# Moving the shifted feed-forward input's transfers behind the scores, and its layer-norm statistics later, in a software-pipelined attention kernel

## The chip, the cores and the metric

The kernel runs on one core of one Trainium2 chip. The metric is the device time of one execution, in microseconds (us). The core has these engines: PE (TensorE, matrix products), DVE (VectorE), ACT (ScalarE), POOL (GpSimd) and SP (SyncE, which here issues nearly all DMA transfers). "PEld" in the profile is PE's weight load, which overlaps its matmuls. Each engine works through its own list of instructions in order; between engines only semaphores order the work, and an engine that waits for one holds up everything behind the wait in its own list.

## What is computed

The input is 2 x 1024 tokens of width 128. The work is: a stack of 6 transformer layers on the normalized input, half of it added; a small recurrent layer in the middle; and the same stack of 6 layers once more. One layer of the stack is (reference, cut down):

```python
def shift_tokens(t):                      # second half of the channels comes from the token before
    a, s = jnp.split(t, 2, -1)
    s = jnp.pad(s, ((0, 0), (1, 0), (0, 0)))[:, :-1]
    return jnp.concatenate([a, s], -1)

def attn_layer(x, Wqkv, qs, ksc, Wo):     # 16 heads of 64, windows of 32 keys looking one window back
    q, k, v = split(x @ Wqkv)
    q, k = l2norm(q) * qs, l2norm(k) * ksc
    q, k = rotary(q), rotary(k)           # with xpos scales
    return local_attention(q, k, v) @ Wo

def ffn_layer(x, g, bln, W1, b1, W2, b2):
    mu = x.mean(-1, keepdims=True)
    var = ((x - mu) ** 2).mean(-1, keepdims=True)
    xn = (x - mu) / jnp.sqrt(var + 1e-05) * g + bln
    hg = xn @ W1 + b1
    a, gate = jnp.split(hg, 2, -1)
    return a * jax.nn.gelu(gate, approximate=False) @ W2 + b2

for i in range(DEPTH):
    x = attn_layer(shift_tokens(x), ...) + x
    x = ffn_layer(shift_tokens(x), ...) + x
```

## The kernel before, in words

The tokens are cut into 16 tiles of 128 (a tile is one SBUF block of 128 partitions), and the residual stream of all of them stays in SBUF, in `Z`. There are 12 layers of 16 tiles, so 192 tile-layers ("tiles" from here on). The program is one software pipeline over these: a *step* is a turn of the pipeline, and in step s the stages work on different tiles. Stage `L_X` (transpose of the input) works on tile s, `L_QKV` on tile s-1, `L_S` (keys, values, scores) on s-2, `L_SM` (softmax) on s-3, `L_AV` and `L_WO` (attention output, output projection) on s-4, `L_F` (first half of the feed-forward part) on s-5 and `L_F2` (its second half) on s-6. All steps are written out, without loops. `k.wait(sem, lag)` waits until the semaphore has counted the tile s-lag; `k.on(lag)` says whether that stage has a tile in this step.

Within a step, each engine's list is written out by hand:

- **PE** (`step`, lines 544 to 658): q/k projection chunks 1 and 0 (L484), transposes of the rotated q (L495), attention times values (L539, 64 matmuls), projection chunks 2 and 3, transposes of the rotated k, output projection (L594), transposes of the probabilities (L602), the transpose of the normalized feed-forward input `xn` (L607, it waits for `a_xn` from ACT), the second feed-forward product (L622), the value projections 1 and 0 (L490), the transpose of the layer's input (L639), the first feed-forward product (L503), and last the scores: the mask (L519) and 128 small matmuls (L527). The last of these signals `p_S`.
- **DVE** (lines 919 to 1021): rotary products of chunks 0 and 1 (L861 and L867, each twice), the row sums of the softmax (L940) and their reciprocals (L949, signals `v_rec` to POOL), sums of squares (L954, L957), the rotary products of chunks 3 and 2, a chain of small operations for the reciprocal square root of the norms (L816 to L848), the two residual additions (L969, signals `v_z1`; L979), a copy of transposed probabilities (L992), the gated product `hT` (L1001), the maximum of the scores (L1008, waits for `p_S`) and their subtraction (L1011, signals `v_sub`).
- **ACT** (lines 679 to 755): squares of chunks 1 and 0 (L673), exponentials (L686), copies of transposed q (L691) and attention output (L695), squares 3 and 2, the copy of transposed k (L711), **`xn`** (L715, waits for `v_nb` from DVE), the copy of transposed probabilities (L722), `xnT` (L727), two value copies (L677), the gelu (L740) and the three parts of the transposed input `xsT` (L747, L748, L750; `a_xT`). PE's first projection of the next step waits for `a_xT`.
- **POOL** (lines 1070 to 1095): the small power for the layer norm (L1074, waits for `v_ve`, signals `g_rstd`), the multiplication of the probabilities by the reciprocals (L1078, waits for `v_rec`, signals `g_nrm` to PE's transposes L602), two additions of rotary products (L1084), a table (L1058), two multiplications by the norms (L1093).
- **SP** (lines 436 to 458): two transfers of the values to `vb` (L447, L448, behind `p_O`), two loads of the next layer's weights in every second step (L357, L361), and the *shift* of the feed-forward input: four transfers (L405 to L408) from `Z` to `xs2`, whose second half of the channels goes down by one partition. They wait for `v_z1` of tile s-4. Each counts 16 on `d_xs2`.

The layer-norm statistics of `xs2` are these: `bn_stats` (L1016) at the end of DVE's list, for tile s-4, behind `d_xs2`; in the next step `bn_aggr` (L932, between the rotary products of chunk 1), the addition of epsilon (L937, signals `v_ve`), POOL's power (L1074), and `nb`, the product of mean and reciprocal deviation (L945, signals `v_nb`), between the row sums and their reciprocals. Then ACT makes `xn` and PE transposes it.

Of the kernel before, what the change touches and what calls it, by code (L numbers as in the profile page):

```python
# [57 lines left out]
def macaron(nc, x_in, w_in, w_out, b_out, w_qkv, q_scale, k_scale, w_o,  # L58
            w_1, w_2, b_2, c_cols, c_rope, c_mask, c_ident, out):
    with ExitStack() as ctx:  # L60
# [293 lines left out]
        def _(sp):  # L354
# [46 lines left out]
            def shift(k, lag, dst, sm):  # L401

                hf, cut = P // 2, P - 16
                new, tail, left = k.slot(lag), k.slot(lag, 0, hf), k.slot(lag, 1, hf)
                sp.dma_start(dst[:, 0:hf], Z[:, bass.ds(new, hf)]).then_inc(sm, 16)  # L405
                sp.dma_start(dst[1:cut + 1, hf:P], Z[0:cut, bass.ds(tail, hf)]).then_inc(sm, 16)
                sp.dma_start(dst[cut + 1:P, hf:P], Z[cut:P - 1, bass.ds(tail, hf)]).then_inc(sm, 16)
                sp.dma_start(dst[0:1, hf:P], Z[P - 1:P, bass.ds(left, hf)]).then_inc(sm, 16)  # L408
# [27 lines left out]
            def step(k):  # L436
                if k.reg is not None:

                    for lag in (L_X, L_WO):
                        k.slot(lag), k.slot(lag, 0, P // 2), k.slot(lag, 1, P // 2)  # L440
                if k.on(L_SM):


                    k.wait(a_v[0], L_SM)
                    k.wait(p_O, L_AV)
                    par = k.parity(L_SM)
                    sp.dma_start(vb[WIN:P, :], va[0:P - WIN, par, :]).then_inc(d_vb, 16)  # L447
                    sp.dma_start(vb[0:WIN, :], va[P - WIN:P, 1 - par, :]).then_inc(d_vb, 16)  # L448
                load_weights(k)
                if k.on(L_WO):  # L450


                    k.wait(v_z1, L_WO)
                    shift(k, L_WO, xs2[:, :], d_xs2)
                if k.reg is None and k.s >= OUT:
                    t = k.s - OUT
                    sp.wait_ge(f_out, t + 1)
                    sp.dma_start(out[t // POS, (t % POS) * P:(t % POS + 1) * P, :], xb[:, t, :]).then_inc(d_out, 16)
# [9 lines left out]
        def _(pe):  # L468
# [75 lines left out]
            def step(k):  # L544
# [52 lines left out]
                if k.on(L_SM):  # L597
# [3 lines left out]
                    for p in range(PAIRS):  # L601
                        last = tr(tps[:, p, :], prob[:, p, :, :].rearrange("p a b -> p (a b)"), idf[:, :])  # L602
                    last.then_inc(p_pT, 1)
                if k.on(L_F):
                    k.wait(a_xn, L_F)
                    k.wait(v_sub, L_S + 1)
                    tr(sps[:, 1, 0:P], xn[:, :], idf[:, :]).then_inc(p_xnT, 1)  # L607
                if k.on(L_F2):
                    if k.reg is None and k.s == L_F2:
                        pe.wait_ge(d_late, 16 * len(late_consts))  # L610
                    k.wait(v_h, L_F2)
                    k.wait(a_oT, L_AV)
                    if k.mid(M_IN) is not None:
                        k.wait_mid(m_xT, M_IN)
                        mm(ops[:, 1, 0:P], winT[:, :], mx_t[:, :], start=True, stop=True, skip_group_check=True)
                    if k.mid(M_OUT) is not None:
                        k.wait_mid(m_y, M_OUT)
                        mm(ops[:, 1, P:2 * P], ys[:, k.mid(M_OUT) % 2, :], woutT[:, :], start=True, stop=True,
                           skip_group_check=True)
                    at = k.layer(L_F2, 3 * P)  # L620
                    for c in range(3):
                        last = mm(ops[:, 1, 3 * P:4 * P], hT[0:FC, c, :], w2[0:FC, bass.ds(at + c * P, P)],  # L622
                                  start=(c == 0), stop=(c == 2))
                    last.then_inc(p_f2, 1)
                if k.on(L_S):
                    weights(k, L_S, d_wq, CHUNKS)
                    k.wait(v_ab[3], L_QKV)
                    values(k, 1)
# [154 lines left out]
        def _(dve):  # L783
# [135 lines left out]
            def step(k):  # L919
                if k.on(L_QKV):  # L920
# [3 lines left out]
                        k.wait(g_tab, L_QKV, base=-1)  # L924
                    rotate(k, 0, True)
                    rotate(k, 0, False)
                if k.on(L_F):
                    k.wait(v_bn, L_F)
                if k.on(L_QKV):
                    rotate(k, 1, True)  # L930
                if k.on(L_F):
                    v.bn_aggr(mv[:, :], st[:, :]).then_inc(v_mv, 1)  # L932
                if k.on(L_QKV):
                    rotate(k, 1, False)
                if k.on(L_F):
                    k.wait(v_mv, L_F)
                    v.tensor_scalar(rt2[:, 0:1], mv[:, 1:2], 1e-5, None, ALU.add).then_inc(v_ve, 1)  # L937
                if k.on(L_SM):
                    k.wait(a_exp, L_SM)
                    v.tensor_reduce(rs[:, :], prob[:, :, :, :].rearrange("p a t j -> p (a t) j"), AX,  # L940
                                    ALU.add).then_inc(v_sum, 1)
                if k.on(L_F):
                    k.wait(g_rstd, L_F)
                    k.wait(a_xn, L_F + 1)
                    v.tensor_scalar(nb[:, 0:1], mv[:, 0:1], rt2[:, 1:2], -1.0, ALU.mult, ALU.mult).then_inc(v_nb, 1)  # L945
                if k.on(L_SM):
                    k.wait(v_sum, L_SM)
                    k.wait(g_nrm, L_SM + 1)
                    v.reciprocal(rr[:, :], rs[:, :]).then_inc(v_rec, 1)  # L949
                if k.on(L_QKV):  # L950
                    k.wait(a_sq[0], L_QKV)
                    k.wait(v_sub, L_S + 1)
                    k.wait(v_rs, L_QKV + 1, per=RS_STEPS)
                    v.tensor_reduce(xsq[:, 0:HEADS], heads(sq[:, 0:INNER]), AX, ALU.add).then_inc(v_red[0], 1)  # L954
                    rotate(k, 3, True)
                    k.wait(a_sq[2], L_QKV)
                    v.tensor_reduce(xsq[:, HEADS:2 * HEADS], heads(sq[:, INNER:2 * INNER]), AX, ALU.add).then_inc(v_red[1], 1)  # L957
                    rotate(k, 3, False)
                    rsqrt(k, 1)
                    rotate(k, 2, True)  # L960
                    rsqrt(k, 2)
                    rotate(k, 2, False)
                    rsqrt(k, 4)
# [41 lines left out]
                if k.on(L_S):  # L1005
# [5 lines left out]
                    v.tensor_tensor(prob[:, :, :, :].rearrange("p a t j -> p t a j"), s4,  # L1011
                                    mx[:, :].rearrange("p (t a) -> p t a", t=2).unsqueeze(3)
                                    .to_broadcast([P, 2, PAIRS, 2 * WIN]), ALU.subtract).then_inc(v_sub, 1)
                if k.on(L_WO):
                    k.wait(d_xs2, L_WO, per=64)
                    v.bn_stats(st[:, :], xs2[:, :]).then_inc(v_bn, 1)  # L1016
                if k.reg is None and k.on(L_F2) and k.tile(L_F2) >= T - TILES:

                    t = k.tile(L_F2) - (T - TILES)
# [33 lines left out]
        def _(pool):  # L1053
# [14 lines left out]
            scl2 = scl[:, :, :, :].rearrange("p l k d -> p (l k d)")  # L1068

            def step(k):  # L1070
                if k.on(L_F):
                    k.wait(v_ve, L_F)
                    k.wait(a_xn, L_F + 1)
                    g_.tensor_tensor(rt2[:, 1:2], rt2[:, 0:1], half[:, 0:1], ALU.pow).then_inc(g_rstd, 1)  # L1074
                if k.on(L_SM):
                    k.wait(v_rec, L_SM)
                    pr = prob[:, :, :, :].rearrange("p a t j -> p (a t) j")
                    g_.tensor_tensor(pr, pr, rr[:, :].unsqueeze(2).to_broadcast([P, HEADS, 2 * WIN]),  # L1078
                                     ALU.mult).then_inc(g_nrm, 1)
                if k.on(L_QKV):  # L1080
                    for g in range(2):
                        k.wait(v_ab[1 + g], L_QKV)
# [147 lines left out]
```

## Time and profile before

| | |
|---|---|
| median of 3 runs | 3302.99 us (3298.94 to 3304.68) |
| the profiled execution's own time | 3302.78 us |
| its span in the trace | 3301.0 us |
| mean granted clock of PE | 0.994 |
| instructions | 125954 |
| busy share of the span | PE 96%, PEld 72%, DVE 91%, ACT 77%, POOL 68% |

The span is the time between the first and the last recorded instruction of this one execution; 1.8 us of its time lie outside it. A busy share is an average over the whole program. A matmul's end is modelled in the trace, so a busy PE is not always a PE at its peak; in rows of several merged instructions the busy time runs from the first start to the last end. "A <- B" in the waits means that the engine at A stood still until B was done; "issue" stands for a wait that the trace ascribes to nothing.

### The profile page before, as it was taken

The numbers are of one execution on the slowest core, as the hardware profiler recorded it, in microseconds if no ns is written. First come the engines' busy times: TensorE is split into PE (matmuls) and PEld (weight loads), VectorE is DVE, ScalarE is ACT, GpSimd is POOL, SyncE is SP. The second block draws the span as 40 slices with busy tenths as digits, with TensorE's granted clock in tenths as the row PEclk, the third lists the DMA queues.
The fourth block names the chain that finished last, engine by engine and source line by source line (L and its number), as shares of the span: only waits on it lengthen the run. The fifth ranks groups of instructions, "written<-read, shape, count | busy, mean of one in ns | idle before, by whom it ended". The sixth has DMA issues, their size and how long they took to land. (4 is left out here: it accounts for less than half of the span.)

```text
span 3301.0 us, 125954 instructions
## 1 busy us (share of the span) xinstructions
PE 3177.7 (96%) x50984; PEld 2377.1 (72%) x51176; DVE 2994.8 (91%) x7143; ACT 2543.2 (77%) x4144; POOL 2229.6 (68%) x1454
## 2 busy tenths in 40 slices
PE   7999999999999999999889999999999999999998
PEld 3777777777777777776667777777777777777776
DVE  7999999999899999999999998899999999999995
ACT  3877878777787777777667777788777777887775
POOL 6666666666666666667777766666666666666663
PEclk9999999999999999999999999999999999999999
DMA  4111111111111111111111111111111111111111
GB/s 124 44 48 44 48 45 48 45 48 44 47 45 48 45 48 45 47 44 39 37 37 47 45 48 45 40 48 46 45 44 48 45 48 45 48 45 48 47 52 38
DMA packets 134996, 155.84 MB, mean 47 GB/s; under 512 B 75539, under 2 KB 108439, under 8 KB 134423
## 3 DMA queue, kind: packets, MB, share of 16 engines
q1 hardware_dynamic: 129815, 144.42, 15.9%
q8 instruction: 413, 6.77, 0.9%
q10 hardware_dynamic: 4608, 3.34, 0.4%
q14 instruction: 160, 1.31, 0.1%
HBM read 33.38 MB, written 1.05 MB: 10 GB/s over the span
## 5 line engine op out<-in xcount | busy, mean ns | idle before, releaser
L1084 POOL TENSOR_TENSOR rot<-rot,swp 128x1024 f32<-128x1024 f32 x384 | 907.2, 2363 | 132.5 <-DVE rot L867 132.5
L484 PE MATMUL proj<-wq,xsT 128*128 128x512 f32 x1536 | 773.4, 622 | 55.9 <-DVE hT L1001 22.4
L673 ACT ACTIVATE sq<-proj 128x512 f32<-128x512 f32 x768 | 437.6, 596 | 400.6 <-PE proj L484 387.3
L1093 POOL TENSOR_TENSOR rot<-rot,rn 128x1024 f32<-128x1024 f32 x384 | 724.6, 1910 | 0.0
L1074 POOL TENSOR_TENSOR rt<-rt,half 128x1 f32<-128x1 f32 x192 | 105.8, 551 | 743.1 <-DVE rt L937 743.1
L861 DVE TENSOR_TENSOR swp<-proj,tab 128x512 f32<-128x512 f32 x768 | 522.0, 680 | 9.4 <-ACT sq L673 5.1
L867 DVE TENSOR_TENSOR rot<-proj,tab 128x512 f32<-128x512 f32 x768 | 518.9, 676 | 1.7 <-PE tps L495 1.6
L495 PEld LDWEIGHTS tps<-idf,rot 128*128 128x128 f32 x3072 | 362.6, 141 | 207.1 <-issue 205.1
L1078 POOL TENSOR_TENSOR prob<-prob,rr 128x1024 f32<-128x1024 f32 x192 | 365.8, 1905 | 174.7 <-DVE rr L949 174.7
L484 PEld LDWEIGHTS proj<-wq,xsT 128*128 128x128 f32 x1536 | 257.5, 189 | 293.0 <-issue 138.1
L495 PE MATMUL tps<-idf,rot 128*128 128x128 f32 x3072 | 402.0, 274 | 3.5 <-POOL rot L1093 1.9
L594 PE MATMUL ops<-wo,oT 128*128 128x128 f32 x3072 | 376.3, 276 | 4.0 <-ACT oT L695 4.0
L539 PE MATMUL ops<-pT,vb 128*64 128x64 f32 x6144 | 379.3, 225 | 0.0
L490 PE MATMUL proj<-wq,xsT 128*128 128x512 f32 x768 | 369.5, 601 | 3.5 <-DVE rot L867 3.3
L539 PE MATMUL ops<-pT,va 128*64 128x64 f32 x6144 | 369.6, 222 | 0.0
L594 PEld LDWEIGHTS ops<-wo,oT 128*128 128x128 f32 x3072 | 359.8, 193 | 4.3 <-issue 4.2
L527 PEld LDWEIGHTS sps<-kT,qT 64*32 64x32 f32 x24576 | 258.4, 105 | 121.5 <-issue 121.1
L722 ACT COPY pT<-tps 64x1024 f32<-64x1024 f32 x192 | 193.2, 1006 | 187.3 <-PE tps L602 187.3
L1001 DVE SCALAR_TENSOR_TENSOR hT<-proj,cols,fg 114x128 f32<-114x128 f32 (+1 forms) x576 | 166.8, 345 | 187.4 <-issue 179.1
L539 PEld LDWEIGHTS ops<-pT,vb 128*64 128x64 f32 x6144 | 311.6, 138 | 32.9 <-issue 32.6
L527 PE MATMUL sps<-kT,qT 64*32 64x64 f32 x24576 | 296.2, 225 | 33.3 <-issue 33.2
L503 PEld LDWEIGHTS proj<-xnT,w 128*114 128x114 f32 (+1 forms) x2304 | 273.5, 178 | 73.7 <-issue 67.9
(104 smaller groups left out, 6164.6 us busy)
## 6 DMA issues: line engine op xcount, KB each, us to landing
vb<-va SPq DMA_DIRECT2D x192, 384.0 KB, 3.5
vb<-va SPq DMA_DIRECT2D x192, 128.0 KB, 3.6
wq<-in_L_ffn_Wqkv SPq DMA_DIRECT2D x95, 192.0 KB, 3.4
xs<-Z SPq DMA_DIRECT2D x192, 32.0 KB
wo<-in_L_ffn_Wo SPq DMA_DIRECT2D x94, 64.0 KB, 2.8
xs<-Z SPq DMA_DIRECT2D x192, 28.0 KB
xs<-Z SPq DMA_DIRECT2D x192, 3.8 KB
xs<-Z SPq DMA_DIRECT2D x192, 0.2 KB
```

What stands on the lines that cost most here:

```text
L484: mm(proj[:, c % 2, :], xsT[:, k.parity(L_QKV), 0:P], wq2[:, bass.ds(w + c * 512, 512)], start=True, stop=True).then_inc(p_qkv[c], 1)
L490: mm(proj[:, c, :], xsT[:, k.parity(L_S), 0:P], wq2[:, bass.ds(w + (4 + c) * 512, 512)], start=True, stop=True).then_inc(p_v[c], 1)
L495: last = tr(tps[:, p, :], rot[:, g * INNER + p * P:g * INNER + (p + 1) * P], idf[:, :])
L527: last = mm(sps[to:to + WIN, ty, p * 64:(p + 1) * 64], qT[rows, p, w * WIN:(w + 1) * WIN], kT[rows, p, at:at + 2 * WIN], start=False, stop ...
L539: last = mm(o4[hp * DH:(hp + 1) * DH, :, g, :], v, pT[:, 2 * p + g, hp, :, :].rearrange("p t i -> p (t i)"), start=True, stop=True, skip_g ...
L594: last = mm(ops[:, 0, 0:P], oT[:, p, :], wo[:, bass.ds(w + p * P, P)], start=(p == 0), stop=(p == PAIRS - 1))
L673: fn(sq[:, c * 512:(c + 1) * 512], proj[:, c % 2, :], ACT.Square).then_inc(a_sq[c], 1)
L861: v.tensor_tensor(halves(swp[:, c * 512:(c + 1) * 512]), swapped, tab[:, bass.ds(po + (2 * g + 1) * POS * DH, DH)] .rearrange("p (a d) -> ...
L867: v.tensor_tensor(heads(rot[:, c * 512:(c + 1) * 512]), heads(src), tab[:, bass.ds(po + 2 * g * POS * DH, DH)].unsqueeze(1) .to_broadcast( ...
L1078: g_.tensor_tensor(pr, pr, rr[:, :].unsqueeze(2).to_broadcast([P, HEADS, 2 * WIN]), ALU.mult).then_inc(g_nrm, 1)
L1084: g_.tensor_tensor(r, r, swp[:, g * INNER:(g + 1) * INNER], ALU.add).then_inc(g_add[g], 1)
L1093: g_.tensor_tensor(r, r, rn[:, g * HEADS:(g + 1) * HEADS].unsqueeze(2) .to_broadcast([P, HEADS, DH]), ALU.mult).then_inc(g_nm[g], 1)
```

## The change

On SP the shift waits for `p_S` of tile s-2 as well, so its four transfers are issued when the scores of the step are done. On PE the transpose of `xn` goes behind the second feed-forward product. On DVE `bn_stats` goes from the end of the step to the next step, behind the four rotary products of chunks 0 and 1 (it now waits for `d_xs2` there); `bn_aggr` comes behind the row sums, the epsilon behind the reciprocals, and `nb` behind the rotary products of chunk 3. On POOL the power comes behind the multiplication of the probabilities.

```diff
@@ SP, step
                     k.wait(v_z1, L_WO)
+                    k.wait(p_S, L_S)
                     shift(k, L_WO, xs2[:, :], d_xs2)
@@ PE, step
-                if k.on(L_F):
-                    k.wait(a_xn, L_F)
-                    k.wait(v_sub, L_S + 1)
-                    tr(sps[:, 1, 0:P], xn[:, :], idf[:, :]).then_inc(p_xnT, 1)
                 if k.on(L_F2):
...
                     last.then_inc(p_f2, 1)
+                if k.on(L_F):
+                    k.wait(a_xn, L_F)
+                    k.wait(v_sub, L_S + 1)
+                    tr(sps[:, 1, 0:P], xn[:, :], idf[:, :]).then_inc(p_xnT, 1)
@@ DVE, step
                     rotate(k, 0, False)
-                if k.on(L_F):
-                    k.wait(v_bn, L_F)
-                if k.on(L_QKV):
                     rotate(k, 1, True)
-                if k.on(L_F):
-                    v.bn_aggr(mv[:, :], st[:, :]).then_inc(v_mv, 1)
-                if k.on(L_QKV):
                     rotate(k, 1, False)
                 if k.on(L_F):
-                    k.wait(v_mv, L_F)
-                    v.tensor_scalar(rt2[:, 0:1], mv[:, 1:2], 1e-5, None, ALU.add).then_inc(v_ve, 1)
+                    k.wait(d_xs2, L_F, per=64)
+                    v.bn_stats(st[:, :], xs2[:, :]).then_inc(v_bn, 1)
                 if k.on(L_SM):
                     k.wait(a_exp, L_SM)
                     v.tensor_reduce(rs[:, :], prob[:, :, :, :].rearrange("p a t j -> p (a t) j"), AX,
                                     ALU.add).then_inc(v_sum, 1)
                 if k.on(L_F):
-                    k.wait(g_rstd, L_F)
-                    k.wait(a_xn, L_F + 1)
-                    v.tensor_scalar(nb[:, 0:1], mv[:, 0:1], rt2[:, 1:2], -1.0, ALU.mult, ALU.mult).then_inc(v_nb, 1)
+                    k.wait(v_bn, L_F)
+                    v.bn_aggr(mv[:, :], st[:, :]).then_inc(v_mv, 1)
                 if k.on(L_SM):
                     k.wait(v_sum, L_SM)
                     k.wait(g_nrm, L_SM + 1)
                     v.reciprocal(rr[:, :], rs[:, :]).then_inc(v_rec, 1)
+                if k.on(L_F):
+                    k.wait(v_mv, L_F)
+                    v.tensor_scalar(rt2[:, 0:1], mv[:, 1:2], 1e-5, None, ALU.add).then_inc(v_ve, 1)
...
                     rotate(k, 3, False)
+                if k.on(L_F):
+                    k.wait(g_rstd, L_F)
+                    k.wait(a_xn, L_F + 1)
+                    v.tensor_scalar(nb[:, 0:1], mv[:, 0:1], rt2[:, 1:2], -1.0, ALU.mult, ALU.mult).then_inc(v_nb, 1)
+                if k.on(L_QKV):
                     rsqrt(k, 1)
...
-                if k.on(L_WO):
-                    k.wait(d_xs2, L_WO, per=64)
-                    v.bn_stats(st[:, :], xs2[:, :]).then_inc(v_bn, 1)
@@ POOL, step
-                if k.on(L_F):
-                    k.wait(v_ve, L_F)
-                    k.wait(a_xn, L_F + 1)
-                    g_.tensor_tensor(rt2[:, 1:2], rt2[:, 0:1], half[:, 0:1], ALU.pow).then_inc(g_rstd, 1)
                 if k.on(L_SM):
                     k.wait(v_rec, L_SM)
...
                                      ALU.mult).then_inc(g_nrm, 1)
+                if k.on(L_F):
+                    k.wait(v_ve, L_F)
+                    k.wait(a_xn, L_F + 1)
+                    g_.tensor_tensor(rt2[:, 1:2], rt2[:, 0:1], half[:, 0:1], ALU.pow).then_inc(g_rstd, 1)
```

## Rows read from the trace of the kernel before

**Rows 1.** The page, busy time, share of the span and instructions of each engine.

```profile
PE 3177.7 (96%) x50984; PEld 2377.1 (72%) x51176; DVE 2994.8 (91%) x7143; ACT 2543.2 (77%) x4144; POOL 2229.6 (68%) x1454
```

**Rows 2.** Two stretches: length; busy us (count) of PE, PEld, DVE, ACT, POOL; PEclk, DMA.

```profile
900.00:1200.00 300.00, 295.38 (x4804) 222.31 (x4819) 274.91 (x653) 240.46 (x390) 203.50 (x127) 1.00 0.17 46
...
1500.00:1800.00 300.00, 273.60 (x4125) 202.55 (x4135) 293.68 (x704) 211.08 (x350) 220.05 (x179) 0.98 0.15 41
```

**Rows 3.** Timeline of steady steps, around PE: start, us, engine, line, operation.

```profile
1004.80 0.68 DVE L867 TENSOR_TENSOR rot<-proj,tab 128x512 f32<-128x512 f32 x1
...
1005.62 0.27 PE L607 MATMUL sps<-idf,xn 128*128 128x128 f32 x1
...
1022.15 0.27 PE L607 MATMUL sps<-idf,xn 128*128 128x128 f32 x1
...
1022.26 0.83 PE L622 MATMUL ops<-w,hT 114*128 114x128 f32 x6
...
1026.76 1.48 PE L527 MATMUL sps<-kT,qT 64*32 64x64 f32 x128
...
1028.05 0.20 ACT L750 ACTIVATE xsT<-xsT 64x1 f32<-64x1 f32 x1
...
1028.35 1.95 PE L484 MATMUL proj<-wq,xsT 128*128 128x512 f32 x4
```

**Rows 4.** Timeline of a steady step, DVE's order from the scores on.

```profile
1012.10 1.23 DVE L1008 TENSOR_REDUCE mx<-sps 128x16 f32<-128x1024 f32 x1
...
1014.01 0.60 ACT L673 ACTIVATE sq<-proj 128x512 f32<-128x512 f32 x1 [0.20 <-PE proj L484]
1014.50 0.28 DVE L1016 BATCH_NORM_STATS2 st<-xs 128x6 f32<-128x128 f32 x1
...
1014.70 0.69 DVE L861 TENSOR_TENSOR swp<-proj,tab 128x512 f32<-128x512 f32 x1
...
1016.59 0.66 DVE L867 TENSOR_TENSOR rot<-proj,tab 128x512 f32<-128x512 f32 x1
...
1018.35 0.21 DVE L945 TENSOR_SCALAR nb<-mv,rt 128x1 f32<-128x1 f32 x1
1018.47 0.25 DVE L949 RECIPROCAL rr<-rs 128x16 f32<-128x16 f32 x1
...
1021.44 0.68 DVE L867 TENSOR_TENSOR rot<-proj,tab 128x512 f32<-128x512 f32 x1
...
1022.04 0.19 DVE L816 TENSOR_SCALAR sps<-sps 128x32 f32<-128x32 f32 x1
```

**Rows 5.** The same step: POOL, and ACT's `xn` and value copies; waits in brackets.

```profile
1017.39 0.55 POOL L1074 TENSOR_TENSOR rt<-rt,half 128x1 f32<-128x1 f32 x1 [3.85 <-DVE rt L937]
...
1018.80 1.90 POOL L1078 TENSOR_TENSOR prob<-prob,rr 128x1024 f32<-128x1024 f32 x1 [0.86 <-DVE rr L949]
...
1020.74 0.52 ACT L715 ACTIVATE xn<-xs,nb,rt 128x128 f32<-128x128 f32 x1
...
1024.06 0.59 ACT L677 COPY va<-proj 128x512 f32<-128x512 f32 x1 [0.35 <-PE proj L490]
...
1024.85 0.59 ACT L677 COPY va<-proj 128x512 f32<-128x512 f32 x1 [0.19 <-PE proj L490]
```

**Rows 6.** SP's transfers: timeline of a steady step.

```profile
1016.96 0.52 SPq L447 DMA_DIRECT2D vb<-va  x1
...
1023.93 0.51 SPq L405 DMA_DIRECT2D xs<-Z  x1
...
1026.01 0.55 SPq L408 DMA_DIRECT2D xs<-Z  x1
```

**Rows 7.** DMA issues: count, KB each, median us from issue to landing.

```profile
vb<-va SPq DMA_DIRECT2D x192, 384.0 KB, 3.5
...
out<-xb SPq DMA_DIRECT2D x16, 64.0 KB, 1.8
```

**Rows 8.** Waits of the whole run: us in total, times, longest.

```profile
DVE mx L1008 <- PE sps L527: 34.2, 34, 2.7
```

## The prediction

> **What bounds the kernel now.** I read the busy shares first. PE is busy 96% of the span, DVE 91%, ACT and POOL well below [rows 1]. Since these are averages, I then read them by stretch. In a steady stretch PE is busy 295.4 of 300 us at full granted clock and DVE 274.9. In the middle, where the recurrent layer is worked in between, DVE is at 293.7 of 300 and PE at 273.6 [rows 2]. So about 176 of the 192 steps belong to PE and about 16 to DVE.
>
> Next I read the timeline of steady steps. PE's two feed-forward transposes L607 are 1022.15 - 1005.62 = 16.5 us apart, which is one step [rows 3]. PE has almost no gap within it, save one at its end: the scores end at 1026.76 + 1.48 = 1028.24, ACT's last part of the transposed input ends at 1028.05 + 0.20 = 1028.25, and PE's next projection starts at 1028.35 [rows 3]. PE thus goes on when ACT has ended, 0.10 us after it. ACT's work ahead of that (value copy, table load, gelu, three copies) starts from PE's value projections. The loop that sets the step is therefore PE from the projections to the values, and from there PE and ACT side by side. The reader should see two things in it: work that only DVE, POOL or SP gain does not shorten a step, and whatever delays PE ahead of its value projections lengthens the step by as much, since ACT's branch starts later too.
>
> **The change, part by part.** All sums are made against the profiled execution, 3302.8 us (span 3301.0 and 1.8 around it), which lies 0.2 us under the median of the runs, so one figure serves for both.
>
> *DVE, the removed bn_stats at the end of the step.* It takes 1014.70 - 1014.50 = 0.20 us from start to start. The rotary product behind it can't move up by that much: it also needs ACT's square, which ends at 1014.01 + 0.60 = 1014.61; with 0.05 us for the signal it starts at 1014.66 in place of 1014.70 [rows 4]. Gain 0.04 us, and it is DVE's alone.
>
> *DVE, up to the last rotary product of chunk 3 (L867 at 1021.44).* bn_stats is added ahead of it (0.20), nb is taken from there (1018.47 - 1018.35 = 0.12), bn_aggr and the epsilon only change places. So that product shifts by -0.04 + 0.20 - 0.12 = +0.04 us [rows 4]. DVE's reciprocals shift by less than 0.05 too: ahead of them bn_stats (0.20) comes, and nb (0.12) and the epsilon, the shorter of the two, go. POOL's multiplication of the probabilities then keeps its place.
>
> *POOL, the power behind the multiplication.* The latter ends at 1018.80 + 1.90 = 1020.70, the power takes 0.55, so g_rstd comes at 1021.25 [rows 5]. nb now stands where L816 starts, at 1022.04, so it finds g_rstd done 0.8 us earlier. POOL's two rotary additions behind it start up to 0.55 us later; POOL is busy 203.5 of 300 us [rows 2] and has that room. Cost nothing; if the 0.8 us were gone, the nb below would be late by the rest.
>
> *nb, xn and PE's transpose: the costly part.* nb starts 0.60 us behind the start of L867 (1022.04 - 1021.44) and takes 0.21; ACT follows after some 0.06, xn takes 0.52, and PE follows 0.10 behind it as above [rows 3 to 5]. From the start of L867 that is 0.04 + 0.60 + 0.21 + 0.06 + 0.52 + 0.10 = 1.53 us. PE's slot for the transpose has moved too, behind six matmuls of (0.83 - 0.28)/5 = 0.11 us each: it comes 0.67 us behind the place of today's L607 [rows 3]. In the one step the transpose is due at 1022.15 + 0.67 = 1022.82 and its input is there at 1021.44 + 1.53 = 1022.97: PE waits 0.15 us. In the other kind of step (every second one has an additional copy on ACT, and PE runs 0.1 us later against DVE) it is due at 1005.62 + 0.67 = 1006.29, the input at 1004.80 + 1.53 = 1006.33: 0.04 us. The mean is 0.095 us, and 176 steps make 17 us. Before, xn was made at 1020.74, a good microsecond ahead of its use, so this cover of PE is what the later statistics take away. Bounds for this term: if all signals come at once (0.06 + 0.10 left out), nothing waits, 0 us; if a weight load of 0.11 us is exposed on top, 0.205 x 176 = 36 us.
>
> *ACT, the later xn.* xn now ends at about 1022.87, and the copy of the probabilities, xnT and the value copies stand behind it. That chain would come some 0.5 us later, but it had waits of 0.35 and 0.19 us for the value projections in it [rows 5], which take that up. I put this at nothing beyond PE's wait; it is inside the upper bound above.
>
> *SP, the shift behind the scores.* Four issues take 1026.01 - 1023.93 + 0.55 = 2.63 us [rows 6]. They now run from 1012.10, where the scores are done [rows 4], to 1014.7; the next thing on SP, the vb transfer at 1016.96 [rows 6], is not held up. The weight loads stand ahead of the shift and stay. When do the transfers land? The last one is issued 2.1 us behind the first, and no row gives its landing: the nearest are 1.8 us (64 KB) and 3.5 us (384 KB) [rows 7], so 3.9 to 5.6 us after the first. bn_stats is due on DVE at 1014.66 + (1016.59 - 1014.70 - 0.09) + 0.57 = 1017.03, 0.09 being bn_aggr that left, so 4.9 us behind 1012.10 [rows 4]. It waits for nothing at the lower end and for 0.7 us at the upper. I take the lower end for most steps, as the transfers are small (at most 32 KB) and thus nearest to the 64 KB row, and the middle, 0.3 us, for those in which something is in the way; as a count of these I take the 34 steps in which PE stopped in the scores for something other than data [rows 8]. That is 10 us, and since nb and xn stand behind bn_stats, it goes to PE in full. Bounds: 0, and 0.7 x 176 = 123 us.
>
> *PE's stops in the scores.* In 34 steps DVE waited 34.2 us in all for the scores [rows 8], 1 us at a time, while these 128 small matmuls went out. The shift's transfers fly just then, at 1023.9 to about 1028 against scores at 1026.8 to 1028.2. If they are the cause, the change gives up to 34 us back. The rows show only that the two are together, so I take nothing: in five of six steps they are together as well and nothing stops. The Trainium skill says in *Runtime: NRT & Kernel Launch*, "Instruction fetch mechanics", that crossing a block of 16 KiB of code costs little and is mostly hidden; by it there would be no such stops, and the trace, with its 34.2 us, disagrees. By that page alone this term would be nothing as well.
>
> *The middle's 16 steps.* DVE's total of work is the same; bn_stats is not late there, since a step lasts longer. Nothing, with 2 us either way.
>
> The sum is +17 + 10 = +27 us: 3302.8 + 27, about 3330.
>
> **The rivals.** *A, forecast: xn reaches PE late.* For it: the path from L867 to the transpose is made of measured parts, and has 0.04 to 0.15 us too little time. Against it: the margin is as small as a signal. 3330; by its bounds 3310 to 3350.
>
> *B: the transfers land late in most steps.* DVE would stand 0.3 to 0.7 us ahead of bn_stats in each step, and PE with it: 0.3 x 176 = 53 us or more on top of A's 17, so 3373 and up. For it: the upper landing row of 3.5 us. Against it: the size of the transfers. It decides from a landing 4.9 us behind the first issue.
>
> *C, faster: the stops in the scores go.* All 34.2 us come back, less A's 17: 3286; with xn on time, 3269. The Trainium skill (*DMA: Bandwidth & Descriptors*, "Queues, rings and completion order") says that a DMA engine takes turns between its queues by whole packets; by that rule a code load does wait behind the shift's packets, and moving them away makes it land earlier. For it: the stops fall exactly on the time of the transfers. Against it: the scores are also the place where PE takes most instructions per microsecond (128 matmuls and their loads in 1.5 us), which alone explains why it would run dry there.
>
> *D: no change.* The signals are quick enough, xn is there in time, and nothing else lies on the loop: 3303, within 6.6 us.
>
> **How the numbers follow.** 0.2% (6.6 us) is about what a measurement of this kernel tells from no change. A 0.56, B 0.10, C 0.18, D 0.16. A's lowest end and D's highest meet, so "same" is 0.16 and slower 0.66. The predicted time is A's. The range takes in A with its bounds, D, the half of C in which only part of the stops goes or A's cost eats it (above 3292), and the beginning of B: 3292 to 3366. For A alone it is 3310 to 3350.
>
> **What would show it.** In the changed profile, PE's or PEld's wait at L607 for ACT's xn should appear with some 15 us in total (it is 4 us in one startup step now), and PE's busy time in a steady 300 us should fall or its count of matmuls with it, by 0.6%. DVE's wait at bn_stats for the transfers would be some tens of steps with 0.1 to 0.7 us; in most steps if B is right. The wait of DVE's maximum for the scores should stay near 34 us; if it falls to a few, C is right. POOL's power should wait less in total, being behind the multiplication. The prediction is wrong if L607 waits for nothing, or if the gap ahead of the next step's projection absorbs what L607 costs.

## The result, and the profile after

The changed kernel takes 3348.3 us (median of 4 runs) against 3303.8 for the kernel before: ratio 1.0139, 95% interval 1.0121 to 1.0156. It is 44 us slower, clear of the noise; the forecast was slower by 27 us, 3330 in a range from 3292 to 3366. The kernel before was run again beside the experiments, and its median there lies between 3304.6 and 3305.5; times are compared with these. All ratios are of fast executions, which leaves out one execution of 7018.6 us, of the run that shortens DVE's stretch.

First the page's busy shares and the two stretches of the windows view after (the columns are those of [rows 1] and [rows 2]):

```profile
PE 3224.6 (96%) x51176; PEld 2380.6 (71%) x51176; DVE 3026.7 (90%) x7143; ACT 2542.8 (76%) x4144; POOL 2222.4 (66%) x1454
```

```profile
900.00:1200.00 300.00, 294.71 (x4772) 218.90 (x4772) 273.00 (x642) 235.20 (x385) 201.88 (x126) 1.00 0.17 45
1500.00:1800.00 300.00, 272.99 (x4131) 201.45 (x4130) 291.34 (x683) 207.14 (x341) 212.52 (x174) 0.95 0.14 38
```

PE's busy share is the same as in [rows 1] although it does the same work in a longer time. The two busy times can't be compared: the trace before lacks 192 matmul records of PE, those of the mask (50984 against 51176). The weight loads are complete in both (51176), so their number in a stretch is the better measure. In the steady stretch it is 4772 against 4819 before [rows 2], 1% fewer, at the same granted clock.

The waits of the whole run after (us in total, times, longest):

```profile
POOL prob L1073 <- DVE rr L943: 1016.4, 192, 13.4
...
ACT xn L716 <- DVE nb L959: 282.1, 192, 4.4
...
PEld proj L491 <- DVE rot L868: 110.0, 186, 1.1
...
DVE mx L1010 <- PE sps L528: 35.6, 37, 2.9
...
PEld sps L625 <- ACT xn L716: 31.6, 107, 1.5
...
DVE st L932 <- DMA xs<-Z: 13.2, 26, 1.7
...
PE sps L625 <- ACT xn L716: 10.6, 28, 1.3
```

ACT now waits in each step for nb, and in 107 steps PE's load waits for xn in turn, as forecast. In 26 steps bn_stats waits for the transfers, 0.5 us each (the line `DVE st <- DMA xs<-Z`). PE's stops in the scores are what they were: 35.6 us against 34.2 [rows 8].

A steady step after, in the timeline, DVE with the rows of the other engines that meet it:

```profile
1030.10 0.60 ACT L674 ACTIVATE sq<-proj 128x512 f32<-128x512 f32 x1 [0.20 <-PE proj L485]
...
1030.78 0.69 DVE L862 TENSOR_TENSOR swp<-proj,tab 128x512 f32<-128x512 f32 x1
...
1033.18 0.28 DVE L932 BATCH_NORM_STATS2 st<-xs 128x6 f32<-128x128 f32 x1
...
1034.79 0.10 DVE L946 TENSOR_SCALAR rt<-mv 128x1 f32<-128x1 f32 x1
1034.82 1.23 DVE L951 TENSOR_REDUCE sps<-sq 128x16 f32<-128x1024 f32 x1
...
1036.81 0.55 POOL L1078 TENSOR_TENSOR rt<-rt,half 128x1 f32<-128x1 f32 x1
...
1037.68 0.68 DVE L868 TENSOR_TENSOR rot<-proj,tab 128x512 f32<-128x512 f32 x1
1038.28 0.21 DVE L959 TENSOR_SCALAR nb<-mv,rt 128x1 f32<-128x1 f32 x1
...
1038.52 0.49 ACT L716 ACTIVATE xn<-xs,nb,rt 128x128 f32<-128x128 f32 x1 [1.57 <-DVE nb L959]
1039.06 0.14 PEld L625 LDWEIGHTS sps<-idf,xn 128*128 128x128 f32 x1 [0.19 <-ACT xn L716]
...
1039.29 0.68 DVE L868 TENSOR_TENSOR rot<-proj,tab 128x512 f32<-128x512 f32 x1
...
1040.02 0.30 PEld L491 LDWEIGHTS proj<-wq,xsT 128*128 128x128 f32 x2 [0.59 <-DVE rot L868]
```

The path of the forecast is there link by link: the last rotary product of chunk 3 at 1037.68, nb at 1038.28, xn at 1038.52, PE's load at 1039.06. But a second one lies beside it. The last rotary product of chunk 2, at 1039.29 to 1039.97, releases PE's load for value projection 0 at 1040.02. From DVE's first rotary product of the step to this one it is 1039.29 - 1030.78 = 8.51 us. Before it was 8.23 us: from 1014.70 [rows 4] to 1022.93, which is this row of the timeline before:

```profile
1022.93 0.68 DVE L867 TENSOR_TENSOR rot<-proj,tab 128x512 f32<-128x512 f32 x1
```

One step can mislead, so here are medians over the same 144 steps of each run's trace (72 on either side of the middle, away from the start and the end). The *stretch* runs from the end of ACT's last square ahead of DVE's first rotary product to the start of the last product of chunk 2. The *step* is the time from one such product to the next; steps of two kinds alternate, and both are given. The runs are those of the experiments below.

| run | stretch, us | step, us (two kinds) |
|---|---|---|
| shortened stretch | 8.08 | 16.34 / 16.44 |
| **before** | 8.37 | 16.37 / 16.45 |
| changed, bn_stats back at the end, shift ahead of the scores | 8.45 | 16.45 / 16.45 |
| before, one more bn_stats at the end | 8.56 | 16.56 / 16.56 |
| before, one more bn_stats behind the products | 8.56 | 16.55 / 16.55 |
| changed, shift ahead of the scores | 8.59 | 16.58 / 16.58 |
| **changed** | 8.59 | 16.59 / 16.58 |
| changed, bn_stats behind the row sums | 8.73 | 16.71 / 16.71 |

In every line but the first, a step takes the stretch and 7.99 us more, within 0.01 us; before, that holds for one kind of step, and the other takes 0.08 us longer than that. So DVE's stretch already set the pace of every second step in the kernel before, and had 0.08 us to spare in the others. In the changed kernel it sets the pace of both kinds: they are 0.22 and 0.14 us longer, 0.18 in the mean, and 0.18 x 176 = 31 us of the 44. The forecast had PE and ACT as the only loop.

### The profile page after: what moved, and what is told of

It is laid out like the page before. It is cut to its first block and busy times, and to the rows that moved or that the text cites. A ratio compares the mean times of both kernels' runs of the same rounds, so it can differ in the third digit from the quotient of the medians.

```text
span 3348.5 us, 126338 instructions
## 1 busy us (share of the span) xinstructions
PE 3224.6 (96%) x51176; PEld 2380.6 (71%) x51176; DVE 3026.7 (90%) x7143; ACT 2542.8 (76%) x4144; POOL 2222.4 (66%) x1454
## 5 line engine op out<-in xcount | busy, mean ns | idle before, releaser
L504 PE MATMUL proj<-xnT,w 128*114 128x128 f32 (+1 forms) x2304 | 311.9, 285 | 2.3 <-ACT xnT L728 1.8
L540 PEld LDWEIGHTS ops<-pT,va 128*64 128x64 f32 x6144 | 312.6, 138 | 0.0
```

The source lines that it names most:

```text
L504: last = mm(proj[0:rows, a, c * P:(c + 1) * P], w1[:, at + a * FH + c * FC:at + a * FH + c * FC + rows], xnT[:, :], start=True, stop=True, ...
L540: last = mm(o4[hp * DH:(hp + 1) * DH, :, g, :], v, pT[:, 2 * p + g, hp, :, :].rearrange("p t i -> p (t i)"), start=True, stop=True, skip_g ...
```

## The experiments

Theory A, the forecast's, was that the late xn costs the time. Its rivals were the place in PE's list (O), the late transfers (L), and PE's stops in the scores (C). All ratios are to the kernel before.

**PE's order alone.** In the kernel before, only this:

```diff
@@ PE, step
-                if k.on(L_F):
-                    k.wait(a_xn, L_F)
-                    k.wait(v_sub, L_S + 1)
-                    tr(sps[:, 1, 0:P], xn[:, :], idf[:, :]).then_inc(p_xnT, 1)
                 if k.on(L_F2):
...
                     last.then_inc(p_f2, 1)
+                if k.on(L_F):
+                    k.wait(a_xn, L_F)
+                    k.wait(v_sub, L_S + 1)
+                    tr(sps[:, 1, 0:P], xn[:, :], idf[:, :]).then_inc(p_xnT, 1)
```

> Before, with PE's transpose of xn alone moved behind the second feed-forward product; everything else as before. Theory A (what costs is that xn comes late from DVE and ACT): xn ends about 1.5 us ahead of its new slot, so PE waits for nothing and the time stays at 3303 +- 5. Rival O (the new place in PE's list costs something by itself: in the changed kernel the place took 0.046 us more ahead of it and 0.056 us more behind it even in the steps without a wait): 0.10 us in each of 176 steps, so 3321.

3308.2 us, ratio 1.0007 (0.9998 to 1.0016). The place costs at most some 5 us; rival O's 18 us fall. In the medians over steps, as in the table, the stretch and both kinds of step are those of the kernel before.

**nb one instruction earlier,** in the changed kernel:

```diff
@@ DVE, step
+                    v.tensor_scalar(nb[:, 0:1], mv[:, 0:1], rt2[:, 1:2], -1.0, ALU.mult, ALU.mult).then_inc(v_nb, 1)
                     rotate(k, 3, False)
-                    v.tensor_scalar(nb[:, 0:1], mv[:, 0:1], rt2[:, 1:2], -1.0, ALU.mult, ALU.mult).then_inc(v_nb, 1)
```

> After, with DVE's nb one instruction earlier, ahead of the last rotary product of chunk 3 (0.6 us) in place of behind it. Theory A: xn ends 0.6 us earlier and PE never waits for it, except where bn_stats itself waited for the transfers; PE's 0.22 us per step go, 39 us in all, save some 5 for the transfers: 3310 to 3316. Rival O: the place in PE's list keeps its 18 us: about 3330. Rival L (the late transfers make the most of it): 3340 or more.

3349.0 us, 1.0134 (1.0120 to 1.0148): nothing gained. That is against theory A and rival O, and inside rival L's "3340 or more", which the next run takes up. Its waits:

```profile
PEld proj L491 <- DVE rot L868: 151.3, 188, 1.1
...
DVE st L932 <- DMA xs<-Z: 13.1, 19, 1.9
...
PEld sps L625 <- ACT xn L716: 2.8, 2, 2.5
```

The wait for xn is gone (31.6 to 2.8 us), and the wait of the very next group of PE's list, the value projections, for DVE's rotary product has grown from 110.0 to 151.3 us, by as much and more. So xn was the first of two waits of about the same length, both behind the same work of DVE. Theory A falls as a theory of the cause. What took its place is theory D: DVE's work between ACT's square and the rotary product of chunk 2 has grown, and this stretch is on the loop.

**The shift ahead of the scores again,** in the changed kernel:

```diff
@@ SP, step
-                    k.wait(p_S, L_S)
                     shift(k, L_WO, xs2[:, :], d_xs2)
```

> After, without SP's wait for the scores; the statistics and PE's order stay as in after. Theory A: DVE's 13 us of waits for the transfers go, and they stood on PE's path: 3335 to 3340. Rival L: 3320 or less. Rival C (the shift's transfers, when they fly with the scores, hold up PE's code): PE's stops in the scores would be longer than in after, so the gain would be given back, 3348 or more.

3336.3 us, 1.0096 (1.0081 to 1.0112): 12 us come back, against 13.2 us of waits for the transfers. Rival L (3320 or less) falls: the late transfers are not the most of it. Rival C falls too, since nothing is given back. The waits for the scores:

```profile
DVE mx L1009 <- PE sps L527: 29.1, 25, 3.0
```

**Both,** in the changed kernel, with the two diffs above:

> After, with both: nb ahead of the last rotary product of chunk 3, and SP's wait for the scores left out. Theory A: neither wait is left, 3303 to 3307. Rival O: 3321. If something third makes the change slow (POOL's or DVE's order), it shows here as what is left above 3303.

3335.1 us, 1.0094 (1.0080 to 1.0108). With neither wait of the forecast left, 30 us of the 44 remain. "Something third" it is. It shows in this wait:

```profile
PEld proj L490 <- DVE rot L867: 144.1, 187, 1.1
```

against 104.0 us before: 40 us more. These are waits of PE's loads, which run ahead of its matmuls, so they tell where PE is held up but are not added up to the time.

**bn_stats back at the end of the step,** in the changed kernel with the shift ahead of the scores; the rest stays:

```diff
@@ DVE, step
                     rotate(k, 1, False)
-                if k.on(L_F):
-                    k.wait(d_xs2, L_F, per=64)
-                    v.bn_stats(st[:, :], xs2[:, :]).then_inc(v_bn, 1)
...
+                if k.on(L_WO):
+                    k.wait(d_xs2, L_WO, per=64)
+                    v.bn_stats(st[:, :], xs2[:, :]).then_inc(v_bn, 1)
```

> After, with SP's wait for the scores left out (as in the run without it, 3336) and bn_stats back at the end of DVE's step; aggregate, epsilon, nb, POOL's order and PE's order stay as in after. Theory D (bn_stats costs because it now stands in DVE's work between ACT's square and the rotary product of chunk 2, which PE's value projection and xn both wait for): 0.2 us of DVE's work leave that stretch, so the 30 us left go, 3303 to 3308. Rival G (the later aggregate, epsilon and power on DVE and POOL make the cost): it stays at about 3330.

3315.1 us, 1.0030 (1.0020 to 1.0041). 21 us of the 31 go with this one instruction; 10 stay. So D holds for the larger part, and a part of G's is there too, though neither gave 3315. Where? The timeline of this run:

```profile
1002.94 0.17 DVE L935 BATCH_NORM_AGGREGATE mv<-st 128x2 f32<-128x6 f32 x1
1003.05 0.25 DVE L939 RECIPROCAL rr<-rs 128x16 f32<-128x16 f32 x1
1003.23 0.10 DVE L942 TENSOR_SCALAR rt<-mv 128x1 f32<-128x1 f32 x1
1003.25 1.23 DVE L947 TENSOR_REDUCE sps<-sq 128x16 f32<-128x1024 f32 x1
1004.39 0.68 DVE L861 TENSOR_TENSOR swp<-proj,tab 128x512 f32<-128x512 f32 x1
```

and the same sum of squares over the whole of its run, then in the kernel before (the view of one line; ns, min/median/max):

```profile
L947 DVE TENSOR_REDUCE sps<-sq x192: 1168/1228/1230, 16.3 to 3258.9; 128x16 f32<-128x1024 f32 x192
```

```profile
L954 DVE TENSOR_REDUCE sps<-sq x192: 1168/1169/1218, 16.3 to 3242.9; 128x16 f32<-128x1024 f32 x192
```

The epsilon stands right ahead of the sum of squares now; the next instruction starts 0.02 us behind it, but the sum takes 59 ns more than where it stood behind the reciprocals. Where in DVE's list a small instruction stands changes what its neighbours take. The whole stretch is 0.08 us longer than before (8.45 against 8.37). That lengthens only those steps that had nothing to spare: 0.04 us in the mean, 7 us in 176 steps. The 18 steps around the middle, where DVE is the bound, took 349.2 us in this run's trace and 342.6 before (one trace each). The two make somewhat more than the 10 us measured.

**nb earlier there as well,** with the same diff as above:

> The run with bn_stats back at the end of the step and no wait for the scores (3315), with nb ahead of the last rotary product of chunk 3 besides. Theory D with the late xn as the second, smaller term: in the 3315 run PE still lost 0.04 us per step at the transpose of xn; these 7 to 10 us go, 3304 to 3308. If the order of epsilon and power costs by itself: 3315.

3313.7 us, 1.0028 (1.0019 to 1.0036). 9 of the 10 us stay. They are not xn's, but the order's.

**A dose of the suspected cost.** Three times the kernel before, with one more bn_stats; nothing of the result depends on it:

```diff
+                if k.on(L_F):
+                    v.bn_stats(sto[:, 0, :], idf[:, :])
```

once behind `bn_stats` at the end of the step:

> Before, plus one more bn_stats of 128 columns (of a constant, into a tile no longer used) at the end of DVE's step, behind the one there. Theory D: DVE's first rotary product waits for ACT's square by only 0.04 us less than for bn_stats, so the place has no room for a second one: 0.16 to 0.2 us per step, 3331 to 3338. Rival S (this place is slack, that is why bn_stats was free there): 3303 to 3310.

once behind `rotate(k, 1, False)`:

> Before, plus the same bn_stats behind the second rotary product of chunk 1, the place of the changed kernel. Theory D: 0.2 us in each of 176 steps, 3335 to 3340, the same as at the end of the step or a little more. Rival S: the cost is that of this place alone, so this one is slower than the one with the extra at the end of the step by 20 us or more.

and once ahead of the gated product:

> Before, plus the same bn_stats ahead of the gated product hT, where DVE waits about 1 us for the gelu. Theory D: hidden, 3303 to 3306. If DVE's sum of work counted anywhere in the step, 0.2 us x 192 = 38 us: 3341. Only the 16 steps of the middle, where DVE is the bound, should show it: 3 us.

At the end 3329.6 us, 1.0071 (1.0059 to 1.0083); behind the rotary products 3329.7, 1.0072 (1.0060 to 1.0083); ahead of the gated product 3308.2, 1.0013 (1.0003 to 1.0023). One bn_stats more costs 25 us in either place of the stretch, and 3 us (1 to 8 by the interval) where DVE waits for the gelu. The three times lie 1 to 5 us outside theory D's ranges, the costly two below them. The table says why: the stretch grew by 0.19 us, one kind of step by nearly as much and the other by 0.11, since it had 0.08 us to spare. That is 0.15 us in the mean, 26 us in 176 steps. Rival S falls: the end of the step is no better place than the new one. In the last of the three it is DVE's wait that shrinks (before, the same wait, in the second fence):

```profile
DVE hT L1003 <- issue: 127.0, 167, 2.7
```

```profile
DVE hT L1001 <- issue: 179.1, 164, 3.0
```

**bn_stats still later,** behind the row sums, in the changed kernel (`bn_stats`, reciprocals, `bn_aggr`, epsilon in this order behind the row sums):

> After (shift behind the scores), with bn_stats behind the row sums in place of ahead of them, 1.2 us later; aggregate behind the reciprocals. Theory D plus late transfers: the transfers have landed by then in nearly all steps, so DVE's 13 us of waits go and the time is that of the run without SP's wait, 3336 +- 4. Rival M (the shift behind the scores costs in another way, for example through the code's own transfers): it stays at 3348.

3355.9 us, 1.0154 (1.0141 to 1.0167). The waits for the transfers are gone from the list, yet the time is 8 us longer, which neither theory had. The timeline says why:

```profile
1016.61 0.23 DVE L940 RECIPROCAL rr<-rs 128x16 f32<-128x16 f32 x1
1016.76 0.15 DVE L943 BATCH_NORM_AGGREGATE mv<-st 128x2 f32<-128x6 f32 x1
1016.94 0.15 DVE L946 TENSOR_SCALAR rt<-mv 128x1 f32<-128x1 f32 x1
1017.05 1.23 DVE L951 TENSOR_REDUCE sps<-sq 128x16 f32<-128x1024 f32 x1
```

The three small operations fill 1017.05 - 1016.61 = 0.44 us here; in the order of the changed kernel, where the reciprocals stand between the two, they fill 1003.25 - 1002.94 = 0.31 us (the rows of the run with bn_stats back). 0.13 us in 176 steps are 23 us; less the 13 us of the transfers' waits that makes +10, and +8 were measured. The medians over steps agree: the stretch and both kinds of step grew by 0.13 us. The epsilon needs the aggregate, which stands right ahead of it here; but it starts 0.18 us behind its neighbour in both orders, so the rows do not show that this need is the cause. PE's wait for xn grew with it (52.2 us, 184 times). So this run fits the transfers' 12 us but doesn't show them by itself; they rest on the run with the shift ahead of the scores, and on the same edit with nb early (3349.0 to 3335.1).

**Shortening the stretch.** In the kernel before, the three small operations of the reciprocal square root between the rotary products of chunks 3 and 2 go behind them:

```diff
                     rotate(k, 3, False)
-                    rsqrt(k, 1)
                     rotate(k, 2, True)
-                    rsqrt(k, 2)
                     rotate(k, 2, False)
-                    rsqrt(k, 4)
+                    rsqrt(k, 1)
...
-                    rsqrt(k, 5)
-                    rsqrt(k, 7)
+                    rsqrt(k, 2)
...
-                    for n in (8, 10, 11, 12):
+                    for n in (4, 5, 7, 8, 10, 11, 12):
                         rsqrt(k, n)
```

> Before, with the three small operations of the reciprocal square root that stand between the rotary products of chunks 3 and 2 (0.29 us in all) moved behind the last product of chunk 2. Theory D: DVE's stretch between ACT's square and that product becomes 0.29 us shorter, PE's wait for it (0.02 us per step) goes, and then PE and ACT bound the step alone: 3297 to 3301. If DVE had slack there: 3303.

3299.0 us, 0.9981 (0.9973 to 0.9990): faster than both kernels, by 0.2% against the one before, and inside the range of theory D.

```profile
DVE hT L998 <- issue: 137.2, 164, 3.0
...
PEld proj L490 <- DVE rot L867: 55.2, 188, 0.8
...
DVE mx L1005 <- PE sps L527: 44.1, 39, 3.2
...
PEld proj L490 <- issue: 41.2, 177, 2.6
```

PE's wait for the rotary product at the value projections falls from 104.0 us, but the same load now waits 41.2 us for nothing that the trace names, where before it was

```profile
PEld proj L490 <- issue: 6.1, 17, 2.6
```

Together that is 96.4 us against 110.1, and not half. The table says why a stretch 0.30 us shorter gives so little: the kind of step that DVE had bound gains 0.03 us, the other nothing, and the step is then 8.26 us and more above the stretch, not 7.99. Here something other than DVE is the bound. PE's stops in the scores were longer (44.1 us against 34.2), but the profile is of the slowest of ten executions (3304.4 us), so this need not be the kernel's.

**And ACT's branch shorter too:** the same, and the copy of the transposed input's first 64 partitions on DVE.

```diff
@@ ACT, step
-                    cp(xsT[0:hf, par, 0:P], ops[0:hf, 0, P:2 * P])
@@ DVE, step
+                if k.on(L_X):
+                    k.wait(p_xT, L_X)
+                    k.wait(p_v[0], L_X + 2)
+                    v.tensor_copy(xsT[0:P // 2, k.parity(L_X), 0:P], ops[0:P // 2, 0, P:2 * P]).then_inc(v_xT, 1)
                 if k.on(L_F):
                     k.wait(p_f[0], L_F)
@@ PE, step
                     k.wait(a_xT, L_QKV)
+                    k.wait(v_xT, L_QKV)
...
                     k.wait(a_xT, L_X + 1)
+                    k.wait(v_xT, L_X + 1)
```

(In the middle's steps ACT's copy of `mx_t` waits for `v_xT` too.)

> As the run before, and the copy of the first 64 partitions of the transposed input goes from ACT to DVE, into DVE's wait for the gelu. Before, PE waited 0.18 us at the end of a step for ACT's last copy. With both DVE's and ACT's branches shorter by 0.25 us, PE's own work is left as the bound: 0.15 to 0.2 us less per step in 176 steps, 3268 to 3277. If only ACT's branch counted, this gain would come without the moved operations as well; if DVE's new copy meets its own bound, less than 10 us.

3311.5 us, 1.0016 (1.0007 to 1.0024): slower than before, not 30 us faster. The profile is of the slowest of the twelve executions (3316.7 us).

```profile
DVE hT L1005 <- issue: 80.7, 167, 3.0
...
PE sps L528 <- issue: 45.2, 41, 2.0
PE proj L485 <- DVE xsT L997: 44.6, 21, 8.3
```

In 21 steps PE waits 44.6 us for the copy that DVE has taken over; 28.9 us in 18 steps of these lie between 1480 and 1850 us, in the middle, where DVE is the bound, and 15.2 in two steps of the start. The mean granted clock was 0.988 to 0.991 in its twelve executions, against 0.992 to 0.995 before. The steady stretches gain less than expected. The windows view, from 300 to 1400 us and from 2000 to 3000, in this run and then before:

```profile
300.00:1400.00 1100.00, 1084.97 (x17724) 817.21 (x17724) 1035.33 (x2457) 868.64 (x1363) 748.83 (x466) 1.00 0.17 46
...
2000.00:3000.00 1000.00, 981.14 (x15971) 739.15 (x15971) 937.59 (x2222) 786.07 (x1233) 675.96 (x420) 1.00 0.17 46
```

```profile
300.00:1400.00 1100.00, 1076.93 (x17507) 809.87 (x17570) 1001.20 (x2381) 874.51 (x1422) 744.66 (x463) 1.00 0.17 46
...
2000.00:3000.00 1000.00, 983.13 (x16038) 739.06 (x16097) 912.19 (x2175) 797.63 (x1300) 681.00 (x423) 1.00 0.17 46
```

By the weight loads, PE gets 0.9% more done in the first stretch and 0.8% less in the second. In the median the two kinds of step are 16.30 and 16.41 us, 0.07 and 0.03 us shorter than before; the rest of the loss was not settled.

What stands behind PE's stops in the scores was not tested, but the traces have a lead. Before, PE stands still for more than 0.7 us within the scores 28 times, and each of these stops ends 2.2 to 2.9 us behind the start of a 16 KB transfer on the queue that the profile calls "instruction". It is the same for the 27 such stops after, and in the three other runs compared (bn_stats ahead of the gated product, shift ahead of the scores, shortened stretch). In steps without a stop the last such transfer lies anywhere from 0 to 12 us back. That fits a load of code that comes too late for PE; it is an argument, not shown.

## Why the prediction was right, and where it was off

The direction and the range were right, the size was 27 us where it is 44. The mechanism was right in part: xn did reach PE late, but taking that wait away gained nothing, because DVE's stretch is itself the loop. Point by point:

- *The shift behind the scores, 10 us:* measured 12 us (3348.3 to 3336.3), with 26 waiting steps of 0.5 us in place of the assumed 34 of 0.3. The sum is near, by two errors that cancel. The forecast took its lower bound, a landing 3.9 us behind the first issue; in the trace after, the median is 4.4 us, and one in ten lands later than 5.4. It was in time in 166 of 192 steps because bn_stats is due 5.1 us behind the first issue in the median, near the 4.9 of the forecast. That the waiting steps would be as many as PE's stops was a guess.
- *PE's stops in the scores, nothing:* right. 34.2 us became 35.6. Rival C is out: the stops don't go when the shift goes. With the shift ahead again and the rest as changed they are 29.1. The Trainium skill (*DMA: Bandwidth & Descriptors*, "Queues, rings and completion order") says that a DMA engine takes turns between its queues by whole packets, so code could wait for the shift's; no run here shows a gain from moving them. The forecast also called the 34.2 us a disagreement with the Trainium skill's "mostly hidden" for a block of code (*Runtime: NRT & Kernel Launch*, "Instruction fetch mechanics"). It is none: the trace before has 413 transfers of 16 KB on the queue called "instruction", and 34 stops, so most such transfers cost nothing there either.
- *POOL's later power, nothing:* right. g_rstd comes at 1036.81 + 0.55 = 1037.36, 0.9 us ahead of nb.
- *bn_stats at the end of the step, a gain of 0.04 us by its removal:* by the rows the square ends at 1030.70 and the product starts at 1030.78, 0.08 us behind and not 0.05, which would make the gain 0.01 us. But the step of [rows 4] is not a typical one: it follows a step of 17.3 us. In the median of the 144 steps the product started 0.16 us behind the square before and 0.09 after, so the gain was 0.07 us.
- *The shift of the last product of chunk 3, +0.04 us:* this term was too small. By the rows, 1037.68 - 1030.78 = 6.90 us now lie between the first rotary product and it, before 1021.44 - 1014.70 = 6.74. That is +0.16 where the forecast's 0.20 - 0.12 gives +0.08; the medians say 6.89 and 6.72. The 0.08 us were lost in the sentence "bn_aggr and the epsilon only change places": the new places cost 0.06 us in the sum of squares alone. From the end of the square, in the median, the product comes 6.98 us later after and 6.88 before, +0.10 in place of +0.04.
- *xn as the costly part, 17 us: this is the step that fell short.* The wait is there, but it isn't the loop. The forecast ended DVE's work at nb, and did not follow it the 1.0 us further to the last product of chunk 2, for which PE's next group waits. That product comes 8.59 - 8.37 = 0.22 us later behind the square. It lengthens the steps by 0.18 us in the mean where the forecast had 0.095 from xn: 31 us in place of 17. The run with nb earlier removed the one wait and none of the time.
- *The loop as PE and ACT alone:* wrong for every second step, as the table shows. There DVE's stretch set the pace already before.
- *The middle's 16 steps, nothing:* about right. The 18 steps around the middle took 342.6 us before and 347.5 after; at 0.18 us a step 3 us of these 5 would have come anyway. The granted clock of the stretch from 1500 to 1800 us was 0.95 in place of 0.98 [rows 2].

The account of the 44 us by differences of medians: the transfers 12 (3348.3 to 3336.3), bn_stats in the stretch 21 (to 3315.1), the order of the small statistics on DVE, POOL and PE 10 (to 3305.0; PE's order alone gave 3 by its median, 5 at most). These are steps down one chain, so they add up by construction; what supports them from outside is the table, with 31 us for the last two, and the one more bn_stats, with 25.

## What to carry to other kernels

When a wait goes and the time stays, look at the next wait behind it on the same engine: two consumers at the end of one producer's stretch hide each other, and only work taken out of the stretch helps. Ask of a small instruction not only how long it takes but where it stands: the same 0.2 us cost 25 us in the loop and 3 us in a wait that was there anyway. And before a loop is named from one step, take the length of many steps against the stretch under suspicion: here two kinds of step alternate, and one engine bound the one and not the other.

## What was not expected of the hardware

- The same sum of squares over 128x1024 took 1169 ns behind the reciprocals and 1228 ns behind the 0.10 us epsilon.
- Two dependent small operations of DVE side by side (aggregate, epsilon) started 0.18 us apart, and the three small ones filled 0.44 us, against 0.31 us with the independent reciprocals between the two. What makes the difference is not known.
- PE's stops within the 128 small matmuls of the scores, about 1 us each, made DVE wait 29.1 to 44.1 us in every run, whether the shift's transfers were in flight or not. The two longest (44.1 and 43.1 us, in the two last runs) come from profiles of the slowest executions of their kernels, and the shortest (29.1) from the fastest one of its kernel.
